# Probabilities times V in windowed attention: V as the stationary operand, two heads in the columns of the array, softmax sums from ScalarE's accumulator

## The reference: what is computed

```python
x = L0_attn_x
xn = _layernorm(x, axis=-1)
s = _L0_attn_ref(xn, ...)            # 4 blocks with a quaternion product, a filter and an MLP
g = _silu(_L0_ffn_ref(xn, ...))      # 8 experts, top 2
x = x + s * g
xn = _layernorm(x, axis=-1)
s = _L1_attn_ref(xn, L1_attn_W_qkv, L1_attn_W_out)
g = _silu(_L1_ffn_ref(xn, ...))      # 32 experts, top 4, and a shared one
x = x + s * g
return x
```

```python
bq = bq * jnp.cos(q_freqs) + rotate_half(bq) * jnp.sin(q_freqs)
bk = bk * jnp.cos(freqs) + rotate_half(bk) * jnp.sin(freqs)
sim = jnp.einsum('bhwid,bhwjd->bhwij', bq, bk)
...
sim = jnp.where(mask, mask_value, sim)
attn = jax.nn.softmax(sim, axis=-1)
out = jnp.einsum('bhwij,bhwjd->bhwid', attn, bv)
out = out.reshape(b, h, n, dh).transpose(0, 2, 1, 3).reshape(b, n, h * dh)
return out @ W_out
```

## Time and profile before

| | us |
|---|---|
| median of 3 runs | 4642.62 |
| profiled execution | 4645.5 |
| its span, first to last instruction | 4643.4 |
| TensorE matmuls busy | 4202.8 (91%) |
| VectorE busy | 3743.4 (81%) |
| ScalarE busy | 3213.5 (69%) |
| GpSimd busy | 2041.7 (44%) |
| mean granted TensorE clock, share of full speed | 0.962 |

### The profile page before, as it was taken

One profiled execution on the slowest core, in us unless ns is written; L12 is line 12 of the kernel. 1 busy time (PEld: TensorE's weight loads), 2 busy tenths in 40 slices (PEclk: granted clock), 3 DMA queues, 4 the chain that ended last, 5 costly groups with the idle time before them and its releaser, 6 DMA issues.

```text
span 4643.4 us, 64247 instructions
## 1 busy us (share of the span) xinstructions
PE 4202.8 (91%) x20080; PEld 2587.5 (56%) x20208; DVE 3743.4 (81%) x8946; ACT 3213.5 (69%) x6111; POOL 2041.7 (44%) x2033
## 2 busy tenths in 40 slices
PE   4769999999999999999999999999999999999979
PEld 3336556565565656555565655656556565655655
DVE  4779788887978889798887978879798887979843
ACT  2447777676776767777676777767777676777745
POOL 1234355444444444454444535444444444545523
PEclk8779999999999999999999999999999999999989
DMA  4011111011111111111111111101111111111100
GB/s 131 14 28 27 29 33 35 25 30 34 29 27 31 33 29 33 28 30 32 29 32 32 27 29 33 35 22 31 33 30 28 30 33 30 27 30 31 35 21 21
DMA packets 144425, 148.30 MB, mean 32 GB/s; under 512 B 27748, under 2 KB 107932, under 8 KB 143960
## 3 DMA queue, kind: packets, MB, share of 16 engines
q1 hardware_dynamic: 144088, 144.19, 11.9%
HBM read 22.45 MB, written 4.19 MB: 6 GB/s over the span
## 4 chain that ended last, share of the span: by engine, by line
PE 36%; DVE 31%; ACT 12%; issue 8%; POOL 8%; SPq 4%; DMA 2%; DVEq 0%; POOLq 0%; ACTq 0%
DVE acc L952 8%; DVE tmp L952 5%; PE bT L1326 5%; PE bU L1364 5%; DVE nmax L1100 4%; PE bC L1371 4%; PE bG L1357 3%; PE bA L1174 3%; PE bT L1158 3%; DVE hu L1139 3%; POOL s_h L644 3%; PE bA L1264 2%; SPq L566 2%; PE bA L1255 2%; DVE tmp L814 2%
## 5 line engine op out<-in xcount | busy, mean ns | idle before, releaser
L644 POOL TENSOR_TENSOR s_h<-s_h,ge 128x512 f32<-128x512 f32 x512 | 700.5, 1368 | 1211.1 <-ACT ge L654 983.4
L952 DVE TENSOR_TENSOR acc<-acc,tmp 128x512 f32<-128x512 f32 x768 | 582.1, 760 | 8.0
L952 DVE TENSOR_TENSOR tmp<-comps 128x512 f32<-128x512 f32 x768 | 579.0, 760 | 8.9
L1371 PE MATMUL bC<-hu,w_d 128*128 128x512 f32 x1056 | 571.1, 623 | 9.1 <-DVE hu L1139 9.1
L776 ACT ACTIVATE s_h<-bG 128x512 f32<-128x512 f32 x528 | 314.8, 596 | 367.1 <-PE bG L1357 187.1
L753 ACT ACTIVATE probs<-bT,nmax 128x256 f32<-128x256 f32 x1024 | 408.1, 474 | 203.5 <-DVE nmax L1100 201.5
L1139 DVE TENSOR_TENSOR hu<-bU,s_h 128x512 f32<-128x512 f32 x528 | 361.7, 685 | 181.3 <-POOL s_h L644 111.4
L631 POOL TENSOR_TENSOR rot<-rot,sinT 128x512 f32<-128x512 f32 x256 | 353.3, 1380 | 297.2 <-DMA rot<-raw 297.1
L1326 PEld LDWEIGHTS bT<-V,probsT 128*128 128x128 f32 x3584 | 430.8, 193 | 83.7 <-issue 43.6
L622 POOL TENSOR_TENSOR comps<-comps 128x255 f32<-128x255 f32 (+1 forms) x384 | 299.1, 779 | 365.3 <-ACT comps L700 365.3
L1326 PE MATMUL bT<-V,probsT 128*128 128x65 f32 x3584 | 442.3, 276 | 14.1 <-ACT probsT L654 12.2
(11 more groups left out here) (201 smaller groups left out, 9363.8 us busy)
## 6 DMA issues: line engine op xcount, KB each, us to landing
rot<-raw SPq DMA_DIRECT2D x1024, 64.0 KB, 2.0
comps<-comps SPq DMA_DIRECT2D x384, 120.0 KB
x_ld<-in_L_attn_x SPq DMA_DIRECT2D x66, 128.0 KB, 2.2
comps<-comps SPq DMA_DIRECT2D x384, 8.0 KB
out<-O SPq DMA_DIRECT2D x16, 256.0 KB, 2.3
w_a<-in_L_attn_W_qkv SPq DMA_DIRECT2D x1, 1536.0 KB, 14.3
w_fc<-in_L_attn_fc_w SPq DMA_DIRECT2D x1, 1024.0 KB, 9.5
w_g<-in_L_ffn_w_gate SPq DMA_DIRECT2D x1, 1024.0 KB, 5.7
```

The lines of the kernel that those rows point to most:

```text
L644: nc.gpsimd.tensor_tensor(s_h[:, :], s_h[:, :], ge[:, :], ALU.mult).then_inc(weighed, 1)
L952: V_.tensor_tensor(dst, i0, i1, op).then_inc(ham[h], 1)
L1371: ins = mm(bC[:, :], down, hu[:, :], start=u in (0, UNITS0), stop=u in (UNITS0 - 1, UNITS - 1))
```

## The change

The step `O` is turned round. V becomes the stationary operand (128 keys by 64 values) and the transposed probabilities the moving one, with up to 256 columns, so the result comes out with the values in the partitions and the tokens in the columns: already the layout of `OT`. Head 0 goes to columns 0 to 63 of the array and to partitions 0 to 63 of the bank, head 1 to columns and partitions 64 to 127. The matmuls of a pair go from 14 to 10: two of 256 columns and two of 128 in the first `O`, two of 256 and four of 128 in the second. The step `OT` and its bank are gone.

The sums no longer come from a column of ones. Each exponential writes its row sum through ScalarE's accumulator (`accum_out`). Two new steps `rinv` per pair follow: VectorE takes the reciprocal of four sums in SBUF; ScalarE copies each of the four over 64 columns (`sums`, 256 columns). TensorE transposes these behind the matmuls of `O`, two transposes per `O`, into the other half of the same bank, and waits for ScalarE's copy to do so. ScalarE then copies that half to SBUF (256 columns), and VectorE multiplies the first half by it, into `OT`. So the bank of an `O` is now read by ScalarE and, after it, by VectorE.

The order of all engines is written anew. Of the table itself one line stands here. Left out are the lists of step names by engine, the two new semaphores `spread` and `scaled`, and the memset of the column of ones, which is gone:

```diff
@@ -68,7 +68,7 @@
     for p in range(HP):
         more = p + 1 < HP
         out += [("q", p + 1), ("k", p + 1)] * more + [("S", p, n) for n in range(4)] + [("rope", p + 1)] * more
-        out += [("PT", p, 0), ("PT", p, 1), ("O", p, 0), ("PT", p, 2), ("PT", p, 3), ("O", p, 1), ("OT", p)]
+        out += [("rinv", p, 0), ("PT", p, 0), ("PT", p, 1), ("rinv", p, 1), ("O", p, 0), ("PT", p, 2), ("PT", p, 3), ("O", p, 1)]
         out += [("V", p + 1)] * more
         if p == 1:
             out += [("gates1_T",)]
...
@@ -124,21 +124,21 @@
 
 STEPS_FOR = {e: {k: [t for t in steps if has_work(e, k, t)] for k, steps in STREAMS.items()} for e in DOES}
 ORDER = {
-    "pe": "uuauabaubauutbtuubuuutttuuutuutuuuuuuttuutuuttuaatutuatuauuatauauatbuuauabauatutbutbubtbubtbtuuu"
-          "utuutbttbubtutuabtuatuttutatatatauattatutttuutttuauatbuabaututututbububububtbtuutututubtbttbtabu"
...
+    "pe": "uuuuaabaubabubutuuttuuttuuuutuuutuuuuuttuuttuuatatuuutatauuataauaubutabuauauuatbuububtbtbttubuut"
...
@@ -255,21 +255,22 @@
         Kk = sb("Kk", [P, S])
         raw = sb("raw", [P, 2, S])
         rot = sb("rot", [P, 2, S])
-        V = sb("V", [P, NW, 2, DH + 1])
+        V = sb("V", [P, NW, 2, DH])
         probs = sb("probs", [P, 2, NW, 2 * WIN])
         probsT = sb("probsT", [P, 2, 4 * WIN])
-        O = sb("O", [P, NW, P])
+        sums = sb("sums", [P, NW, P])
         OT = sb("OT", [P, 2, S])
         y = sb("y", [P, S])
         nmax = sb("nmax", [P, 2, NW])
-        rinv = sb("rinv", [P, 2, 2])
+        rsum = sb("rsum", [P, NW, 2])
+        rinv = sb("rinv", [P, NW, 2])
         s_h = sb("s_h", [P, S])
         ge = sb("ge", [P, S])
         hu = sb("hu", [P, S])
         gate1_f = sb("gate1_f", [P, S])
         gates1 = sb("gates1", [PARTS * E1, S], bf16)
         x1n = rot[:, 0, :].rearrange("p (t d) -> p t d", t=NT)
-        y_out = O
+        y_out = sums
         stB, mvB = sb("stB", [P, NT, 6]), sb("mvB", [P, NT, 2])
         veB, rsB = sb("veB", [P, NT]), sb("rsB", [P, NT])
         r1_s = sb("r1_s", [P, NT, E1])
...
@@ -744,22 +744,27 @@
                         copy(raw[:, "qk".index(t[0]), :], b[:, :]).then_inc(t_sem(t), 1)
                     if t[0] == "V":
                         t_ready(act, r, t)
-                        copy(V[:, :, :, 0:DH], b[:, :].rearrange("p (w h d) -> p w h d", w=NW, h=2)).then_inc(t_sem(t), 1)
+                        copy(V[:, :, :, :], b[:, :].rearrange("p (w h d) -> p w h d", w=NW, h=2)).then_inc(t_sem(t), 1)
                     if t[0] == "S":
                         h = t[2] % 2
                         act.wait_ge(smax, r.b * (NW * HP) + (NW * t[1] + t[2] + 1))
                         for k in range(2):
                             w = t[2] // 2 * 2 + k
                             ins = nc.scalar.activation(probs[:, h, w, :], b[:, k * 2 * WIN:(k + 1) * 2 * WIN], ACT.Exp,
-                                                       bias=nmax[:, h, w:w + 1])
+                                                       bias=nmax[:, h, w:w + 1], accum_out=rsum[:, w, h:h + 1])
                         ins.then_inc(t_sem(t), 1)
                     if t[0] == "PT":
                         t_ready(act, r, t)
                         at = P if t[2] < 2 else 0
                         copy(probsT[:, t[2] % 2, at:], b[:, at:]).then_inc(t_sem(t), 1)
-                    if t[0] == "OT":
+                    if t[0] == "rinv":
+                        w = slice(2 * t[2], 2 * t[2] + 2)
+                        act.wait_ge(rinved, r.b * (2 * HP) + (2 * t[1] + t[2] + 1))
+                        copy(sums[:, w, :].rearrange("p w (h d) -> p w h d", h=2),
+                             rinv[:, w, :].unsqueeze(3).to_broadcast([P, 2, 2, DH])).then_inc(spread, 1)
+                    if t[0] == "O":
                         t_ready(act, r, t)
-                        copy(OT[:, t[1] % 2, :], b[:, :]).then_inc(t_sem(t), 1)
+                        copy(sums[:, 2 * t[2]:2 * t[2] + 2, :].rearrange("p w d -> p (w d)"), b[:, HT:S]).then_inc(scaled, 1)
                     if t[0] == "gates1_T":
                         t_ready(act, r, t)
                         copy(gates1[:, :], b[:, :].bitcast(bf16)[0:PARTS * E1, 0:S]).then_inc(t_sem(t), 1)
@@ -1099,17 +1104,17 @@
                         w, h = t[2] // 2 * 2, t[2] % 2
                         V_.tensor_reduce(nmax[:, h, w:w + 2], b[:, :].rearrange("p (w n) -> p w n", w=2), AX.X, ALU.max,
                                          negate=True).then_inc(smax, 1)
+                    if t[0] == "rinv":
+                        w = slice(2 * t[2], 2 * t[2] + 2)
+                        if t[1:] == (0, 0):
+                            dve.wait_ge(stored, r.b * 16 + 16)
+                        for k in range(2):
+                            t_ended(dve, r, ("S", t[1], 2 * t[2] + k))
+                        V_.reciprocal(rinv[:, w, :], rsum[:, w, :]).then_inc(rinved, 1)
                     if t[0] == "O":
-                        n = 2 * t[1] + t[2] + 1
-                        w = range(2 * t[2], 2 * t[2] + 2)
-                        if (t[1], t[2]) == (0, 0):
-                            dve.wait_ge(stored, r.b * 16 + 16)
-                        t_ready(dve, r, t)
-                        out4 = b[:, 0:4 * (DH + 1)].rearrange("p (w h d) -> p w h d", w=2, h=2)
-                        V_.reciprocal(rinv[:, :, :], out4[:, :, :, DH]).then_inc(rinved, 1)
-                        dve.wait_ge(rinved, r.b * (2 * HP) + n)
-                        V_.tensor_tensor(O[:, w[0]:w[0] + 2, :].rearrange("p w (h d) -> p w h d", h=2), out4[:, :, :, 0:DH],
-                                         rinv[:, :, :].unsqueeze(3).to_broadcast([P, 2, 2, DH]),
+                        dve.wait_ge(scaled, r.b * (2 * HP) + (2 * t[1] + t[2] + 1))
+                        V_.tensor_tensor(OT[:, t[1] % 2, t[2] * HT:(t[2] + 1) * HT], b[:, 0:HT],
+                                         sums[:, 2 * t[2]:2 * t[2] + 2, :].rearrange("p w d -> p (w d)"),
                                          ALU.mult).then_inc(t_sem(t), 1)
                     if t[0] == "out":
                         l = t[1]
@@ -1294,8 +1299,7 @@
                     b = t_bank(t)
                     builds_on = {"route1": [("xn1_T",)], "PT": [("S",) + t[1:]],
                                  "O": [("V",) + t[1:2]] + [("PT", t[1], 2 * t[-1] + k) for k in range(2)] if t[0] == "O" else [],
-                                 "OT": [("O",) + t[1:] + (k,) for k in range(2)],
-                                 "out": [("OT", 2 * t[-1] + k) for k in range(2)] if t[0] == "out" else []}
+                                 "out": [("O", 2 * t[-1] + k, n) for k in range(2) for n in range(2)] if t[0] == "out" else []}
                     if t == ("q", 0):
                         builds_on["q"] = [("xn1_T",)]
                     t_begin(pe, r, t, *builds_on.get(t[0], []))
@@ -1319,15 +1323,14 @@
                         tiles = [probs[:, h, first_w + w, k * P:(k + 1) * P] for w in range(2) for k in range(2)]
                         ins = transposes(b[:, skip * P:], tiles[skip:])
                     if t[0] == "O":
-                        for w in range(2):
+
+                        tiles = ((2, 1, 0, 2), (1, 0, 0, 1), (3, 3, 1, 1)) if t[2] else ((0, 1, 0, 2), (1, 3, 1, 1))
+                        for n, (key, at, to, wide) in enumerate(tiles):
                             for h in range(2):
-                                keys = (0, 1) if t[2] or w else (1,)
-                                for k in keys:
-                                    ins = mm(b[:, (2 * w + h) * (DH + 1):(2 * w + h + 1) * (DH + 1)],
-                                             probsT[:, h, (2 * w + k) * P:(2 * w + k + 1) * P],
-                                             V[:, 2 * t[2] + w + k - 1, h, :], start=k == keys[0], stop=k == 1)
-                    if t[0] == "OT":
-                        ins = transposes(b, [O[:, w, :] for w in range(NW)])
+                                mm(b[h * DH:(h + 1) * DH, to * WIN:(to + wide) * WIN], V[:, key, h, :],
+                                   probsT[:, h, at * WIN:(at + wide) * WIN], start=n == 0, stop=n == len(tiles) - 1)
+                        pe.wait_ge(spread, r.b * (2 * HP) + (2 * t[1] + t[2] + 1))
+                        ins = transposes(b[:, HT:S], [sums[:, 2 * t[2] + w, :] for w in range(2)])
                     if t[0] == "gates1_T":
                         pe.wait_ge(r1_done, r.b + 1)
                         bank = b[:, :].bitcast(bf16)
```

38 lines of the change are left out of this document (19 added, 19 removed).

## The result

The changed kernel takes 4654.42 us (median of 14 runs, 4646.64 to 4661.6), the kernel before 4643.38 us in as many runs beside it. The ratio is 1.0023, with a 95% interval of 1.0015 to 1.003: slower by 11 us, where 69 us less were forecast. The sign was wrong, and the forecast 80 us too low; the time lies inside the range.

The account below looks back on a forecast made before the run. Taken to bound the kernel: TensorE and VectorE, both close to full, passing the pace in fixed order. TensorE -92 and ScalarE +23 gave -69 us: 4576.5 profiled, 4574 as median; range 4490 to 4675.

Parts of the forecast that it names:

- TensorE, the overlap: In step `O`, two heads in different array columns overlap: 1.93 us per pair, 267 us in all with factor 1.08.
- The rival without overlap: In `O`, head 1 runs after head 0: 416 us, a saving of only 26, total 4652 us; chance 0.14.
- The transposes, taken as 0: Four transposes of `O` become four of `sums`, same size, so no change in TensorE time: 0.
- TensorE, the switch of width: Going between full-width and half-width matmuls around `O` costs nothing that can be seen, judged from the scores.
- the draining rival: Each switch at `O` drains the array: 512 x 0.16 = 82 us, 43 on the path, 4617 us; chance 0.10.
- the scores' factor 0.64: Scores, two heads in the rows: 1.10 us instead of 1.72 one after another; applied to the new `O`.
- TensorE, size and share on the path: Rewritten `O` matmuls save 175 us of TensorE, 0.52 of it on the path: 92 us.
- What is removed from ScalarE: ScalarE loses the 128 `OT` copies, 76 us, and 75 table loads, 96 us, priced at share 0.17.
- What is added to ScalarE: ScalarE gains two copies, 106 and 98 us, and accumulators at 0.1 us each, 102 us, at share 0.17.
- The slower rival: ScalarE binds at the exponentials: 247 us more, half on the path, 124 against 92, 4675 us; chance 0.16.
- VectorE: 0: VectorE's reciprocal and multiplication keep their length, and its moved waits come out even: 0.
- Waits at `sums<-rinv`: ScalarE's wait for the reciprocal is covered by a table load and Silu; otherwise 140 us, 24 on the path.

Follow-up runs that it names:

- t_before: Kernel before, with GpSimd's two long in-place multiplications cut to 2 of 512 columns: 4533.1 us.
- t_newO: Kernel before with only the new product, in its old order, and GpSimd's two long multiplications cut to 2 of 512 columns: 4476.8 us.
- t_bare: Changed kernel without accumulators, reciprocals and both new ScalarE copies, GpSimd's two long multiplications cut to 2 of 512 columns: 4484.8 us.
- t_after: Changed kernel, with GpSimd's two long in-place multiplications cut to 2 of 512 columns: 4553.2 us.
- b_newO: Kernel before, in its own order, with only the new product; output not the reference's: 4588.7 us.
- a_oldO: Changed kernel with its product put back to 14 matmuls of the old form, 64 columns each; output not the reference's: 4718.6 us.
- b_neword: b_newO with the steps of all engines put in the changed kernel's order: 4784.8 us.

## Why the prediction was wrong, by its steps

With few collisions the change can be added up in three pieces, each a difference of two runs, and set beside the prediction's:

| step | predicted | measured |
|---|---|---|
| the product (t_before to t_newO) | -92 | -56 |
| new order; 75 table loads, the `OT` copy and the old reciprocals gone (t_newO to t_bare) | 0.17 x (-76 - 96) = -29 | +8 |
| accumulators, reciprocals in SBUF, two copies (t_bare to t_after) | 0.17 x (106 + 98 + 102) = +52 | +68 |
| sum | -69 | +20 |

With all of GpSimd's work the sum is +11.

*TensorE, the overlap: right.* 1.82 us per pair (forecast 1.93), 253.8 us of L1330 (forecast 267). The rival without overlap is refuted, by the starts in the timeline. The transposes, taken as 0, are 34.5 us more by their group, two at a time instead of four; what that is worth wasn't tried.

*TensorE, the switch of width: put at nothing, wrongly.* "The switch costs nothing that can be seen" came from a misreading of the earlier trace rows. The matmul whose 0.31 us to the next start served as the measure has 24 rows (24*128) and pays for a switch itself; one with 96 rows and the same 512 columns takes 0.22 (2087.84 to 2088.06 above). In the trace of before, the mask's last matmul takes 0.31 us until the scores begin (median of 256), and 0.22 where a full-width matmul follows it (median of 108). So the draining rival exists, at 0.09 us instead of 0.16. For 512 switches that is some 47 us of TensorE's time. The half on the way out was in the scores' factor 0.64 and so in the forecast; the half on the way in, up to 24 us, was not.

*TensorE, size and share on the path: the first error, 36 us.* "On the path, 0.52 x 175 = 92 us" has both factors too large. Counted as above, TensorE as a whole lost 143 us from t_before to t_newO (4074.2 to 3931.6), not 175; the way into half width is up to 24 us of the difference, the rest wasn't traced. At 0.52 this is 17 us of the error. Of the 143, 56 came out, 0.39: the other 19 us. "232 / 442.3 = 0.52 of its time is on the path" took the share of the lines in the chain of before for what their removal is worth, but the chain says only who was last. In b_newO VectorE takes the places (31% to 40% of the chain). That isn't the whole answer: with few collisions L1326 has 7.2% of the chain of t_before, 326 us or 0.73 of its busy time, VectorE has only 24% of that of t_newO, and still no more than 56 us came out. Why the share is so much smaller there stays open.

*What is removed from ScalarE: the second error, 37 us.* The load and copy savings were credited at ScalarE's average share of 0.17. t_bare has 148 us less of ScalarE's work than t_newO and is 8 us slower. The same piece holds the rewritten order, which the prediction priced at nothing, and with it VectorE is busy for 25 us more in t_bare, with 40 us of reciprocals gone, which looks like collisions. The +8 by itself can't be told from nothing; the 29 us that were forecast are clearly not there. What the loads alone are worth isn't separated from it.

*What is added to ScalarE: mis-sized, 16 us.* The accumulator was bounded rightly at 0 to 0.21 us and taken at 0.1; it costs 0.09 of issue and 0.203 of latency. ScalarE's added time is smaller than the 306 us forecast, 3300.8 - 3065.3 = 235.5, but 68 us for it is a share of 0.29, not 0.17. My reading, which no run shows by itself: this work stands in one chain, exponential, sum, reciprocal, copy, transpose, copy, product, and isn't average work. The slower rival named this place (exponentials) and "92 / 247 = 0.37 of ScalarE's time"; neither its share nor its size (247 us) was reached. The result came from half-way, a smaller gain met by a smaller loss; that it lies within the stated range is luck.

*VectorE: 0 was wrong in kind.* Its busy time rose by 29.5 us, through no instruction of its own. "I take these as even", of its waits, was wrong too: it waits 87.3 us for `sums` and 89 us more for the scores, against 59 us saved.

*Waits at `sums<-rinv`: right.* 34.8 us, not among the largest, so the cover that the order promised was there.

No version that gives the reference's output beat the kernel before. The lead is b_newO: the old order and steps with the new product, 55 us faster; what it lacks is a way to bring the sums to the product's layout for less than that. This wasn't built.

## What to carry to other kernels

A line's share of the chain of work overstates what shortening the line is worth. In the three tests here (shares of 0.52, 0.72 and 0.73 of the line's own time in before, a_oldO and t_before, times 186, 191 and 194 us) 0.57, 0.46 and 0.40 of that product came out: expect about half. Take the saving from the whole engine's busy time, not from the group's. Where work is added inside one dependent chain (here between exponential and output), price it at a higher share than the engine's average (here 0.29 against 0.17). And read an untouched engine's mean instruction times after any reordering: if they moved, two engines may collide, and an experiment's gain or loss may be theirs.

## What the runs showed of the hardware

- An accumulator output on ScalarE is a second instruction, 203 ns, of which 0.09 us adds to the distance between exponentials of 256 columns (0.46 us against 0.37).
- A switch between full-width matmuls and those on half of the array, in the rows or in the columns, costs about 0.09 us on the way in and on the way out (0.522 instead of 0.429 us after 512 columns, 0.203 instead of 0.111 after 128). The modelled ends hide it; it is seen in the distance between starts.
- Two float32 matmuls in different columns of the array overlap: 1.82 us for what would stream in 3.01 one after another, a factor of 0.60, a little better than the two heads in the rows (0.64). Both hold the way out; without it they are 0.54 and 0.59.
- VectorE instructions with two SBUF inputs, and its single-input ones from SBUF to SBUF (L940, up to 1.39 us instead of 0.285), alternate with GpSimd's by whole instructions. Between b_newO and b_neword VectorE's busy time for the same instructions goes from 3741 to 3924 us; with GpSimd's long ones cut, from 3555 to 3661.
- Between the order of b_newO and that of b_neword lie 196 us, 4.3%, at the same work but for 75 table loads fewer in the slower one: more than the change itself gained or lost.
